# Half-height transposes and a state product on four 64x64 places of TensorE, with a new plan of PSUM banks

## The chip, the cores and the metric

One NeuronCore of a Trainium2 chip runs the whole kernel in one launch. It has five engines that run side by side and signal each other through semaphores: TensorE (matrix products, PE in the profile, its weight loads PEld), VectorE (DVE), ScalarE (ACT), GpSimd (POOL) and SyncE (SP, here for DMAs). TensorE writes only to PSUM, which has eight banks of 512 float32 values in each of 128 partitions; VectorE and ScalarE read it from there. The metric is the time of one execution on the device in microseconds; the kernel before takes 1892.21 us, median of 3 runs from 1891.94 to 1892.32.

## The reference

All data is float32. `x` has 4 sequences of 2048 tokens and 256 channels. A block with a gated linear recurrence (16 heads, state 64 x 64) is followed by a layer norm, a coupled feed-forward part with three cycles, and another layer norm:

```
xn = layernorm(x) * gamma + beta
Q, K, V = xn @ WQ.T + bQ, ...              # 16 heads of 64
gate = silu(xn @ Wg.T + bg)
h_t = alpha * h_{t-1} + k_t v_t^T ;  o_t = q_t^T h_t      # per head, over 2048 tokens
x1 = layernorm(x + x + (o * gate) @ WO.T + bO)
gf = sigmoid(mlp3(mean over tokens of x1))
out = x1
3 times: tf = sigmoid(mlp4(out)); coupling = 0.1 + range * (0.7 gf + 0.3 tf - 0.5) * 2
         out = out + coupling * twist(out)   # channel halves swapped with signs
result = layernorm(x1 + out)
```

## The kernel before

**Tiling.** Each sequence (`b`) is worked in four steps (`s`, counted through as `it`) of 512 tokens; a step is four chunks (`c`) of 128 tokens. Heads go in pairs `p` = 0 to 7; the two heads `e` of a pair lie on partitions 0 to 63 and 64 to 127. `n = it * 8 + p` counts head pairs through, 128 in all.

**A head pair** on TensorE: `project` makes keys, queries and gates of the next pair (6 matmuls of 512 columns each, float32 split into a high and a low part); `y_part` adds the output projection of the pair before; `from_state` multiplies the queries with the state at each chunk's start; `keys_transposed` turns the decayed keys `k_end` to tokens; `from_chunk` adds the masked scores times values; `updates` makes each chunk's addition to the state, of the next pair; `scores` makes the next pair's scores. Before the eight pairs, `values` projects V in eight parts. Plain float32 products run as two matmuls each, transposes as one.

**The other engines.** VectorE evacuates keys (`keys_of`, L615) and queries (`queries_of`, L624), masks the scores (`masked`, L703), runs the state from chunk to chunk (L732, L736) and multiplies the result with the gate (`gated`, L714). ScalarE makes the scaled, block-diagonal state `h_bd` (`states_of`, L454), shifted queries (L436), the gate (L428) and the copy `k_tok` of the transposed keys (L446); around the steps it scales the transposed x (L420), splits it (L423) and copies x1 (L462). GpSimd makes `k_end` (L362).

**What sets the order.** Every engine's program is written out by hand in the order in which it runs; waits are on counting semaphores, each with one meaning (`state_carried` is the last state step, `k_evacuated` the keys out of PSUM, `gate_evacuated` the gate). A bank is written again only after its reader signalled, so the plan of banks decides which waits there are. Before, keys and queries alternate between banks 0 and 1, the gate is in the keys' bank, scores are in 2 and 3, transposed keys and state updates in 4, the result of the scan in 5, the output projection in 6 and 7. x is transposed into banks 0 and 1 behind the keys of p = 6. In the feed-forward part (`order`, layers 1 to 4) L1078, L1095, L1108 and L1121 are the four layers, L934 transposes x1, and L943 turns the final sum back.

## Time and profile before

| | |
|---|---|
| median of the runs | 1892.21 us |
| profiled execution | 1892.58 us |
| its span, first to last instruction | 1890.8 us |
| mean granted TensorE clock | 0.985 of full speed |
| PE busy | 1824.6 us, 96% |
| PEld busy | 1396.9 us, 74% |
| DVE busy | 1062.4 us, 56% |
| ACT busy | 699.9 us, 37% |
| POOL busy | 312.9 us, 17% |

The busy time of an engine is the union of its instructions' times; the ends of matmuls are modelled, and they are pipelined, so that their times overlap each other. PE and PEld are the same engine, its matmuls and its weight loads. One group of the table of costliest groups is one source line with one kind of operands; it gives busy time, mean time of one instruction, and the idle time of the engine ahead of them. The chain that ended last runs 94% over PE.

### The profile page before, as it was taken

To read this page: it belongs to the slowest core of one execution; us is meant where nothing else is said; L and a number is where in the kernel's file an instruction comes from. 1 tells how busy PE (TensorE), PEld (TensorE's weight loads), DVE (VectorE), ACT (ScalarE), POOL (GpSimd) and SP (SyncE) were. 2 spreads that over 40 slices of the span, in tenths; PEclk is the share of its full clock that TensorE was granted. 3 is DMA by queue.
4 is the path that set the end of the run, shared out by engine and by line. 5 is a ranking of instruction groups with operands and counts; after the bars stand their busy time and mean duration, and the time that the engine had idled before them with its cause. 6 is when DMAs were issued, how large, how long until landed. Compare 5 with 4: busy or idle time off the path is not lost.

```text
span 1890.8 us, 43949 instructions
## 1 busy us (share of the span) xinstructions
PE 1824.6 (96%) x19120; PEld 1396.9 (74%) x19120; DVE 1062.4 (56%) x2214; ACT 699.9 (37%) x1282; POOL 312.9 (17%) x244
## 2 busy tenths in 40 slices
PE   5999999999899999999989999999989999999996
PEld 4888888863588888885368888888437888888732
DVE  7565555555745555554665645555565555555556
ACT  3323333344433333334433332323443333233344
POOL 4121211102212121110221112121022111212002
PEclk8999999999899999999989999999999999999998
DMA  4000000000100000000010000000001000000001
GB/s 161 2 13 2 13 2 12 2 1 1 56 2 13 2 12 2 12 2 1 0 57 2 13 2 13 2 13 2 1 1 57 2 13 2 13 2 2 2 0 45
DMA packets 22817, 26.11 MB, mean 14 GB/s; under 512 B 3169, under 2 KB 21473, under 8 KB 22625
## 3 DMA queue, kind: packets, MB, share of 16 engines
q1 hardware_dynamic: 20624, 19.09, 3.2%
q10 hardware_dynamic: 2000, 4.20, 0.6%
q8 instruction: 152, 2.49, 0.6%
q14 instruction: 41, 0.33, 0.1%
HBM read 14.90 MB, written 8.39 MB: 12 GB/s over the span
## 4 chain that ended last, share of the span: by engine, by line
PE 94%; DVE 3%; ACT 2%; POOL 1%; issue 0%; DMA 0%; ACTq 0%; DVEq 0%; SPq 0%
PE bank L848 39%; PE bank L923 12%; PE bank L1078 9%; PE bank L911 7%; PE bank L875 6%; PE bank L902 6%; PE bank L1095 4%; PE bank L892 3%; PE bank L884 3%; PE bank L1121 1%; PE bank L1108 1%; DVE stats L582 1%; PE bank L839 1%; DVE v_sb L816 1%; PE bank L934 1%; DVE x_nf L809 1%
## 5 line engine op out<-in xcount | busy, mean ns | idle before, releaser
L714 DVE TENSOR_TENSOR o_g<-bank,gate 128x512 f32<-128x512 f32 x128 | 88.6, 692 | 484.6 <-PE bank L911 484.6
L362 POOL TENSOR_TENSOR k_end<-k_sc,pows 128x512 f32<-128x512 f32 x128 | 134.9, 1054 | 1075.6 <-DVE k_sc L615 1075.6
L436 ACT ACTIVATE q_sb<-q_sb,pows 128x384 f32<-128x384 f32 (+2 forms) x384 | 167.3, 498 | 331.6 <-DVE q_sb L624 331.6
L454 ACT ACTIVATE h_bd<-h_seq,pows 64x256 f32<-64x256 f32 x256 | 129.9, 507 | 323.5 <-DVE h_seq L736 320.3
L923 PE MATMUL bank<-wo,o_g 128*128 128x256 f32 x1024 | 243.5, 380 | 0.8 <-DVE o_g L714 0.8
L923 PEld LDWEIGHTS bank<-wo,o_g 128*128 128x128 f32 x1024 | 192.7, 190 | 32.9 <-DVE o_g L714 1.0
L446 ACT ACTIVATE k_tok<-bank 128x512 f32<-128x512 f32 x128 | 76.5, 598 | 299.9 <-PE bank L884 299.9
L703 DVE COPY_PREDICATED att<-causal,bank 128x1024 f32<-128x1024 int32 x128 | 167.3, 1307 | 6.2 <-PE bank L875 5.4
L911 PE MATMUL bank<-att,v_sb 128*64 128x128 f32 x2048 | 140.1, 279 | 0.0
L902 PEld LDWEIGHTS bank<-q_sb,h_bd 128*128 128x128 f32 x1024 | 134.1, 191 | 7.4 <-ACT h_bd L454 0.2
L902 PE MATMUL bank<-q_sb,h_bd 128*128 128x128 f32 x1024 | 134.9, 275 | 0.0
L875 PE MATMUL bank<-q_sb,k_sc 64*32 64x128 f32 (+3 forms) x8192 | 128.1, 236 | 0.0
L911 PEld LDWEIGHTS bank<-att,v_sb 128*64 128x64 f32 x2048 | 109.2, 136 | 24.4 <-issue 24.3
L624 DVE SCALAR_TENSOR_TENSOR q_sb<-bank,col_bias,pows 128x512 f32<-128x512 f32 x128 | 96.2, 751 | 53.9 <-PE bank L848 53.4
L736 DVE SCALAR_TENSOR_TENSOR h_seq<-h_seq,pows,bank 128x64 f32<-128x64 f32 x384 | 107.9, 281 | 24.3 <-PE bank L892 1.9
L1078 PE MATMUL bank<-v_sb,f_w 128*128 128x512 f32 x256 | 121.0, 605 | 0.0
L848 PE MATMUL bank<-x_hi,wk_hi 128*128 128x512 f32 x256 | 114.6, 448 | 0.0
L875 PEld LDWEIGHTS bank<-q_sb,k_sc 64*32 64x32 f32 x8192 | 102.1, 106 | 14.3 <-issue 5.9
L696 DVE TENSOR_TENSOR v_sb<-bank,bias_v 128x512 f32<-128x512 f32 x128 | 85.1, 688 | 47.4 <-PE bank L848 46.8
L848 PE MATMUL bank<-wv_hi,x_hi 128*128 128x512 f32 x256 | 108.5, 424 | 2.4 <-POOL wv_lo L358 1.7
L848 PE MATMUL bank<-x_hi,wq_hi 128*128 128x512 f32 x256 | 102.9, 402 | 3.4 <-DVE x_lo L610 3.4
L848 PE MATMUL bank<-x_hi,wg_hi 128*128 128x512 f32 x256 | 103.6, 405 | 2.2 <-POOL wg_lo L358 2.2
(137 smaller groups left out, 3213.6 us busy)
## 6 DMA issues: line engine op xcount, KB each, us to landing
x_in<-in_x SPq DMA_DIRECT2D x16, 512.0 KB, 4.3
out_y<-q_sb SPq DMA_DIRECT2D x8, 512.0 KB, 2.8
out_y<-x_nf SPq DMA_DIRECT2D x8, 512.0 KB, 3.1
v_sb<-in_wq ACTq DMA_DIRECT2D x1, 1024.0 KB, 5.2
v_sb<-in_wk SPq DMA_DIRECT2D x1, 1024.0 KB, 9.0
x1t<-in_wg ACTq DMA_DIRECT2D x1, 1024.0 KB, 9.4
x1t<-in_wv ACTq DMA_DIRECT2D x1, 1024.0 KB, 13.5
wo<-in_wo ACTq DMA_DIRECT2D x1, 1024.0 KB, 17.4
```

Of the source, the lines that this page charges most:

```text
L362: nc.gpsimd.tensor_tensor(k_end[:].rearrange("p (a z) (b r) -> p a (z b) r", z=2, r=BL), k_sc[:].rearrange("p (a z) (b r) -> p a (z b) r", ...
L436: last = nc.scalar.activation(q_sb[:, p % 2, d].rearrange("p (a z) n -> p a (z n)", z=2)[:, :, reach], q_sb[:, p % 2, 0].rearrange("p (a z ...
L454: nc.scalar.activation(h_bd[rows, :, e * DH:(e + 1) * DH], h_seq[rows, :, :], ACT.Copy, scale=pows[rows, p, HP:HP + 1]).then_inc(s_hbd, 1)
L624: nc.vector.scalar_tensor_tensor(q_sb[:, p % 2, 0].rearrange("p c (b r) -> p (c b) r", r=BL), bank[q_bank(p)].rearrange("p (c r) -> p c r" ...
L703: nc.vector.copy_predicated(att[:].rearrange("p e (a z) n -> p (e a) (z n)", z=2), causal[:].bitcast(i32).rearrange("p z n -> p (z n)").un ...
L736: step = nc.vector.scalar_tensor_tensor(h_seq[:, c + 1, :] if c + 1 < NC else h_st[:, p, :], h_seq[:, c, :], pows[:, p, HP + 1:HP + 2], ba ...
L848: last = nc.tensor.matmul(dst, l(k), r(k), start=(m == 0), stop=(m == 5))
L875: last = nc.tensor.matmul(bank[2 + e][g * BL:(g + 1) * BL, cols:cols + count * BL], k_sc[rows, c, g * BL:(g + 1) * BL], query_blocks(rows, ...
L902: nc.tensor.matmul(bank[5][:, c * C:(c + 1) * C], h_bd[:, c, :], query_blocks(slice(0, P), p, c, first, NB), start=(c == 0), stop=False, s ...
L911: last = nc.tensor.matmul(bank[5][e * DH:(e + 1) * DH, c * C:(c + 1) * C], v_sb[:, c, h * DH:(h + 1) * DH], att[:, e, c, :], start=False, ...
L923: last = nc.tensor.matmul(dst, o_g[:, p % 2, tok], wo[:, p, :], start=(p == 0 and c % 2 == 0), stop=(p == NP - 1), skip_group_check=True)
L1078: last = nc.tensor.matmul(l1_bank(j, m)[:], f_w1[:, k, m * P:(m + 1) * P], src[:, k, tile_cols(t)], start=(k == 0), stop=(k == KT - 1))
```

## The change

- **State product.** `from_state` multiplies 64 rows with 64 columns for each head and chunk in place of a block-diagonal 128 x 128. Head `e` of an even chunk writes partitions `e * 64` up of bank 4; in odd chunks the two heads' halves are swapped and in bank 5, so the four products of two chunks lie on the four 64x64 places of the array. The state is scaled in one activation to `h_sc`, without zero blocks. `from_chunk` writes to the same places, the gate of odd chunks is written with its halves swapped, and the output projection takes `wo` with swapped halves for them (two more DMAs of half of `wo` at the start).
- **Transposes.** Every 128 x 128 transpose becomes two of 64 rows by 128 columns (`by_halves`), row half `e` into bank `first_bank + e`; the readers take their columns from two banks.
- **Banks.** Keys, gate and one half of the transposed keys use bank 0; queries, the other half and the state updates bank 1; V uses banks 2 to 5; x is transposed into banks 2 and 3, ahead of `y_part` of p = 6.

```diff
-            return n % NP % 2 if n else 5
+            return 0 if n else 5
+        def head_half(c, e):
+            first = (e + c) % 2 * DH
+            return slice(first, first + DH)
+        def halves_of(first_bank, first, count):
+            return psum[:, first_bank:first_bank + 2, first * DH:(first + count) * DH].rearrange(
+                "p r (c n) -> p c r n", n=DH)
...
-            return bank[(2, 3, 5, 1, 2, 3, 0, 5)[m]]
+            return bank[2 + m % 4]
...
-                nc.scalar.activation(gate[:, p % 2, :], bank[g_bank(n)], ACT.Silu,
-                                     bias=col_bias[:, 2, p:p + 1]).then_inc(s_gev, 1)
+                even, odd = by_places(bank[g_bank(n)])[:, 0], by_places(bank[g_bank(n)])[:, 1]
+                nc.scalar.activation(by_places(gate[:, p % 2, :])[:, 0], even, ACT.Silu, bias=col_bias[:, 2, p:p + 1])
+                for e in range(2):
+                    rows, other = slice(e * DH, (e + 1) * DH), slice((1 - e) * DH, (2 - e) * DH)
+                    last = nc.scalar.activation(by_places(gate[other, p % 2, :])[:, 1], odd[rows], ACT.Silu,
+                                                bias=col_bias[rows, 2, p:p + 1])
+                last.then_inc(s_gev, 1)
...
-                nc.scalar.activation(k_tok[:], part(bk, NC), ACT.Copy).then_inc(s_ktok, 1)
+                nc.scalar.activation(in_halves(k_tok[:].rearrange("p c m -> p (c m)")), halves_of(0, 0, NC),
+                                     ACT.Copy).then_inc(s_ktok, 1)
...
-                for e in range(2):
-                    rows = slice(e * DH, (e + 1) * DH)
-                    nc.scalar.activation(h_bd[rows, :, e * DH:(e + 1) * DH], h_seq[rows, :, :],
-                                         ACT.Copy, scale=pows[rows, p, HP:HP + 1]).then_inc(s_hbd, 1)
+                nc.scalar.activation(h_sc[:], h_seq[:], ACT.Copy, scale=pows[:, p, HP:HP + 1]).then_inc(s_hsc, 1)
...
+                act.wait_ge(s_x1t, step + 1 + C0)
                 for k in range(KT):
-                    act.wait_ge(s_x1t, step * KT + k + 1 + C0)
...
+                            if p == NP - 2 and following:
+                                x_scaled(it + 1)
+                            tokens_of(n + 1)
...
-                nc.vector.tensor_tensor(o_g[:, p % 2], bank[5], gate[:, p % 2, :], ALU.mult).then_inc(s_og, 1)
+                nc.vector.tensor_tensor(by_places(o_g[:, p % 2]), psum[:, 4:6, 0:2 * C].rearrange("p z (a n) -> p z a n", n=C),
+                                        by_places(gate[:, p % 2, :]), ALU.mult).then_inc(s_og, 1)
...
+            def by_halves(first_bank, place, src):
+                for e in range(2):
+                    rows = slice(e * DH, (e + 1) * DH)
+                    last = nc.tensor.transpose(bank[first_bank + e][:, place * DH:(place + 1) * DH],
+                                               src[rows, :], ident[rows, rows])
+                return last
...
-                    last = nc.tensor.transpose(bank[bk][:, c * C:(c + 1) * C], k_end[:, c, :], ident[:])
+                    last = by_halves(0, c, k_end[:, c, :])
...
-                    nc.tensor.matmul(bank[5][:, c * C:(c + 1) * C], h_bd[:, c, :],
-                                     query_blocks(slice(0, P), p, c, first, NB),
-                                     start=(c == 0), stop=False, skip_group_check=True)
+                    place = slice(c // 2 * C, (c // 2 + 1) * C)
+                    for e in range(2):
+                        rows = slice(e * DH, (e + 1) * DH)
+                        nc.tensor.matmul(bank[4 + c % 2][head_half(c, e), place], h_sc[rows, c, :],
+                                         query_blocks(rows, p, c, first, NB),
+                                         start=(c < 2), stop=False, skip_group_check=True)
...
-                            pe.wait_ge(s_qev, n + 1 + C0)
-                            project("k", p + 1, k_bank(p + 1)).then_inc(s_k, 1)
-                            pe.wait_ge(s_gev, n + 1)
-                            project("q", p + 1, q_bank(p + 1)).then_inc(s_q, 1)
+                            project("k", p + 1, 0).then_inc(s_k, 1)
+                            pe.wait_ge(s_hend, n + 1 + C0)
+                            project("q", p + 1, 1).then_inc(s_q, 1)
...
+                        if p == NP - 2 and following:
+                            pe.wait_ge(s_xn, it + 2)
+                            pe.wait_ge(s_att, n + 1 + C0)
+                            x_transposed()
...
                             pe.wait_ge(s_kend, n + 2 + C0)
-                            pe.wait_ge(s_hend, n + 1 + C0)
-                            keys_transposed(4).then_inc(s_kt, 1)
+                            pe.wait_ge(s_qev, n + 2 + C0)
+                            pe.wait_ge(s_gev, n + 2)
+                            keys_transposed().then_inc(s_kt, 1)
...
-                                pe.wait_ge(s_x1c, (b + 1) * NS * KT - 1 + j + C0)
+                                pe.wait_ge(s_x1c, (b + 1) * NS * KT + C0)
```

The order of the instructions shows it at three places. A row is line, operation, output and inputs, the output's shape, the count of equal ones in a row, and the semaphores waited for. First TensorE in p = 0 of the first step, before: the ends of the key and query projections (`wk`, `wq`), the starts behind them, and what follows the gate projection (`wg`).

```order
L848 MATMUL bank<-x_hi,wk_lo 128x512
L848 MATMUL bank<-x_hi,wq_hi 128x512 [waits gate_evacuated]
L848 MATMUL bank<-x_lo,wq_hi 128x512
...
L848 MATMUL bank<-x_hi,wq_lo 128x512
L848 MATMUL bank<-x_hi,wg_hi 128x512 [waits k_evacuated]
...
L848 MATMUL bank<-x_hi,wg_lo 128x512
L902 MATMUL bank<-q_sb,h_bd 128x128 [waits o_gated,state_diagonal_ready]
L902 MATMUL bank<-q_sb,h_bd 128x128 x3
L884 MATMUL bank<-ident,k_end 128x128 [waits state_carried,k_end_ready]
L884 MATMUL bank<-ident,k_end 128x128 x3
```

The same place after:

```order
L876 MATMUL bank<-x_hi,wk_lo 128x512
L876 MATMUL bank<-x_hi,wq_hi 128x512 [waits state_carried]
L876 MATMUL bank<-x_lo,wq_hi 128x512
...
L876 MATMUL bank<-x_hi,wq_lo 128x512
L876 MATMUL bank<-x_hi,wg_hi 128x512 [waits k_evacuated]
...
L876 MATMUL bank<-x_hi,wg_lo 128x512
L933 MATMUL bank<-q_sb,h_sc 64x128 [waits o_gated,state_scaled]
L933 MATMUL bank<-q_sb,h_sc 64x128 x7
L860 MATMUL bank<-ident,k_end 128x64 [waits gate_evacuated,q_evacuated,k_end_ready]
L860 MATMUL bank<-ident,k_end 128x64 x7
```

The wait of the query projection went from the gate to the state, the key transposes wait for gate and queries instead of the state, and the state product is twice as many of half the rows. TensorE in p = 6, before, from the output projection (`wo`) to the state updates (L892):

```order
L923 MATMUL bank<-wo,o_g 128x256 [waits o_gated]
L923 MATMUL bank<-wo,o_g 128x256 x3
L902 MATMUL bank<-q_sb,h_bd 128x128 [waits o_gated,state_diagonal_ready]
L902 MATMUL bank<-q_sb,h_bd 128x128 x3
L884 MATMUL bank<-ident,k_end 128x128 [waits state_carried,k_end_ready]
L884 MATMUL bank<-ident,k_end 128x128 x3
L839 MATMUL bank<-ident,x_nf 128x128 [waits gate_evacuated,q_evacuated,x_n_ready]
L839 MATMUL bank<-ident,x_nf 128x128 x7
L911 MATMUL bank<-att,v_sb 64x128 [waits scores_masked]
L911 MATMUL bank<-att,v_sb 64x128 x7
```

After:

```order
L860 MATMUL bank<-ident,x_nf 128x64 [waits scores_masked,x_n_ready]
L860 MATMUL bank<-ident,x_nf 128x64 x15
L955 MATMUL bank<-wo,o_g 128x256 [waits o_gated]
L955 MATMUL bank<-wo,o_g 128x256 x3
L933 MATMUL bank<-q_sb,h_sc 64x128 [waits o_gated,state_scaled]
L933 MATMUL bank<-q_sb,h_sc 64x128 x7
L860 MATMUL bank<-ident,k_end 128x64 [waits gate_evacuated,q_evacuated,k_end_ready]
L860 MATMUL bank<-ident,k_end 128x64 x7
L943 MATMUL bank<-att,v_sb 64x128 [waits scores_masked]
L943 MATMUL bank<-att,v_sb 64x128 x7
```

The x transposes stand ahead of the output projection and wait for the masked scores. ScalarE in p = 0, from the state (`h_bd`, `h_sc`) to `k_tok`, before:

```order
L454 ACTIVATE h_bd<-h_seq,pows 64x4x64 [waits o_ready,state_step]
L454 ACTIVATE h_bd<-h_seq,pows 64x4x64
L436 ACTIVATE q_sb<-q_sb,pows 128x2x192 [waits q_evacuated]
L436 ACTIVATE q_sb<-q_sb,pows 128x2x128
L436 ACTIVATE q_sb<-q_sb,pows 128x2x64
L428 ACTIVATE gate<-bank,col_bias 128x512 [waits gate_projected,o_gated]
L446 ACTIVATE k_tok<-bank 128x512 [waits state_update_ready,k_end_transposed]
```

After:

```order
L471 ACTIVATE h_sc<-h_seq,pows 128x256 [waits o_ready,state_step]
L454 ACTIVATE q_sb<-q_sb,pows 128x2x192 [waits q_evacuated]
L454 ACTIVATE q_sb<-q_sb,pows 128x2x128
L454 ACTIVATE q_sb<-q_sb,pows 128x2x64
L442 ACTIVATE gate<-bank,col_bias 128x2x128 [waits gate_projected,o_gated]
L445 ACTIVATE gate<-bank,col_bias 64x2x128 x2
L464 ACTIVATE k_tok<-bank 128x512 [waits state_update_ready,k_end_transposed]
```

One activation makes the state where two did, and three the gate where one did.

## Rows read from the trace of the kernel before

**Rows 1.** Page, part 1: engine, busy us (share), instructions.
```profile
PE 1824.6 (96%) x19120; PEld 1396.9 (74%) x19120; DVE 1062.4 (56%) x2214; ACT 699.9 (37%) x1282; POOL 312.9 (17%) x244
```

**Rows 2.** Waits table: engine, line, awaited; us in total, times, longest.
```profile
PEld bank L848 <- DVE k_sc L615: 8.4, 23, 0.4
```

**Rows 3.** Timeline, head pair p = 5: start us, us, engine, line, shapes, count.
```profile
190.20 1.89 PE L923 MATMUL bank<-wo,o_g 128*128 128x256 f32 x8
191.00 0.67 ACT L428 ACTIVATE gate<-bank,col_bias 128x512 f32<-128x512 f32 x1
...
191.92 1.05 PE L902 MATMUL bank<-q_sb,h_bd 128*128 128x128 f32 x8
...
192.81 0.60 PE L884 MATMUL bank<-ident,k_end 128*128 128x128 f32 x4
...
193.34 1.09 PE L911 MATMUL bank<-att,v_sb 128*64 128x128 f32 x16
193.45 0.60 ACT L446 ACTIVATE k_tok<-bank 128x512 f32<-128x512 f32 x1 [1.78 <-PE bank L884]
194.16 0.60 PEld L892 LDWEIGHTS bank<-v_sb,k_tok 128*64 128x64 f32 x16
194.27 0.63 PE L892 MATMUL bank<-v_sb,k_tok 128*64 128x64 f32 x16
```

**Rows 4.** Groups by shape: busy us, mean ns of one, idle before.
```profile
L703 DVE COPY_PREDICATED att<-causal,bank 128x1024 f32<-128x1024 int32 x128 | 167.3, 1307 | 6.2 <-PE bank L875 5.4 <-issue 0.2
...
L902 PE MATMUL bank<-q_sb,h_bd 128*128 128x128 f32 x1024 | 134.9, 275 | 0.0
...
L892 PE MATMUL bank<-v_sb,k_tok 128*64 128x64 f32 x2048 | 82.1, 222 | 2.3 <-ACT k_tok L446 2.3
...
L884 PE MATMUL bank<-ident,k_end 128*128 128x128 f32 x512 | 76.8, 273 | 0.0
...
L436 ACT ACTIVATE q_sb<-q_sb,pows 128x256 f32<-128x256 f32 x128 | 63.0, 492 | 0.0
L884 PEld LDWEIGHTS bank<-ident,k_end 128*128 128x128 f32 x512 | 60.7, 141 | 2.2
...
L436 ACT ACTIVATE q_sb<-q_sb,pows 128x128 f32<-128x128 f32 x128 | 49.4, 386 | 0.0
...
L1121 PEld LDWEIGHTS bank<-x_2b,f_w 64*128 64x128 f32 x96 | 7.2, 184 | 21.9 <-issue 15.2 <-ACT x_2b L541 6.7
```

**Rows 5.** Timeline: the scores, eight places of 64x32.
```profile
205.55 1.00 PE L875 MATMUL bank<-q_sb,k_sc 64*32 64x128 f32 x64
```

**Rows 6.** Timeline: row halves side by side, then transposes without and with a change.
```profile
203.09 1.04 PE L839 MATMUL bank<-ident,x_nf 128*128 128x128 f32 x8
...
419.26 0.30 PEld L1121 LDWEIGHTS bank<-x_2b,f_w 64*128 64x128 f32 x4 [0.76 <-issue]
419.26 1.13 PE L1121 MATMUL bank<-x_2b,f_w 64*128 64x512 f32 x4
...
482.24 1.09 PE L943 MATMUL bank<-ident,v_sb 128*128 128x128 f32 x8
```

**Rows 7.** Timeline, head pair p = 0.
```profile
231.09 0.40 PE L848 MATMUL bank<-x_hi,wq_hi 128*128 128x512 f32 x1
...
231.61 1.04 ACT L454 ACTIVATE h_bd<-h_seq,pows 64x256 f32<-64x256 f32 x2 [5.67 <-DVE h_seq L736]
231.61 0.28 DVE L736 SCALAR_TENSOR_TENSOR h_st<-h_seq,pows,bank 128x64 f32<-128x64 f32 x1
...
233.54 1.31 ACT L436 ACTIVATE q_sb<-q_sb,pows 128x384 f32<-128x384 f32 x3 [0.89 <-DVE q_sb L624]
...
233.87 0.39 PE L848 MATMUL bank<-x_hi,wg_lo 128*128 128x512 f32 x1
...
234.76 0.67 ACT L428 ACTIVATE gate<-bank,col_bias 128x512 f32<-128x512 f32 x1
...
234.99 0.60 PE L884 MATMUL bank<-ident,k_end 128*128 128x128 f32 x4
```

More of the change, by code:

```diff
@@ L98, in build @@
         h_seq = sb("h_seq", [P, NC, DH])
-        h_bd = sb("h_bd", [P, NC, P])
+        h_sc = sb("h_sc", [P, NC, DH])
         o_g = sb("o_g", [P, 2, ST])
@@ L838, in x_transposed @@
                     for c in range(NC):
[L839 to L841 removed]
+                        last = by_halves(2, k * NC + c, x_n[:, c, k * P:(k + 1) * P])
+                last.then_inc(s_xt, 1)
             def products(dst, first, end, l_hi, l_lo, r_hi, r_lo):
@@ L922, in y_part @@
                     dst = bank[6 + c // 2][:, (c % 2) * D:(c % 2 + 1) * D]
-                    last = nc.tensor.matmul(dst, o_g[:, p % 2, tok], wo[:, p, :], start=(p == 0 and c % 2 == 0),
+                    last = nc.tensor.matmul(dst, o_g[:, p % 2, tok], wo[:, c % 2, p, :], start=(p == 0 and c % 2 == 0),
                                             stop=(p == NP - 1), skip_group_check=True)
@@ L933, in x1_transposed @@
                     for c in range(NC):
-                        last = nc.tensor.transpose(bank[first_bank + k][:, c * C:(c + 1) * C],
-                                                   x_n[:, c, k * P:(k + 1) * P], ident[:])
-                    last.then_inc(s_x1t, 1)
+                        last = by_halves(first_bank, k * NC + c, x_n[:, c, k * P:(k + 1) * P])
+                last.then_inc(s_x1t, 1)
             def final_transposed(b, t):
```

123 lines of the change are left out of this document (57 added, 66 removed).

## The prediction

> **What bounds the kernel now.** I read the page's first lines, then the waits, then the order of time inside one head pair, then the groups by shape. TensorE's matmuls are busy 1824.6 of 1890.8 us [rows 1]. That alone proves little, since the ends of pipelined matmuls are modelled, so the waits come next: the largest wait of TensorE on another engine inside the scan is its weight load waiting for the evacuated keys, 8.4 us in 23 places [rows 2]. So in the eight head pairs of each 512-token step TensorE works without a gap, and a microsecond taken from it is won unless another engine's result then comes late. The timeline shows the stretch that changes, in the usual head pair (p = 1 to 5) [rows 3]: `y_part` (L923), product with the state (L902), transposed keys (L884), product with the masked scores (L911), state update (L892). Each starts before the modelled end of the one ahead. ScalarE's gate (ends 191.67) has more than a microsecond before the transposes; its `k_tok` (ends 194.05) has only 0.1 us before L892's weights load (194.16).
>
> **Step times.** From the timeline and the means by shape [rows 3, 4]: L902 is 8 matmuls in 1.05 us, so (1.05 - 0.275) / 7 = 0.111 us from start to start; L884 (0.60 - 0.273) / 3 = 0.109 us for 128 columns; L892, two column places side by side, (0.63 - 0.22) / 7 = 0.058 us per pair of 64 columns; L911, also two places, 0.109 us per pair of 128 columns. Time thus goes with the columns streamed, and places run side by side: with eight places 64 matmuls take 1.00 us [rows 5], 16 ns apart on average. A change of tile shape costs: within one shape the next group starts 0.16 us before the modelled end of the last (L902 ends 192.97, L884 starts 192.81), across shapes only 0.07 us before (L884 ends 193.41, L911 starts 193.34), and its first weight load is uncovered. An uncovered load of a plain 128-column operand is 0.11 us (the second pair of L1121's loads starts 0.30 - 0.184 = 0.11 us after the first [rows 4, 6]). A transpose's load is shorter, 141 ns against the 184 of L1121's 128 columns [rows 4], and uncovered it costs 0.05 us (L943 behind a change of shape 1.09 us, L839 without one 1.04, both 8 transposes [rows 6]); a 64-column load is the same 0.05.
>
> **The state product, 128 times.** Before, 4 block-diagonal products are 8 matmuls, 8 x 0.111 = 0.89 us. Now 8 products of 64x64 are 16 matmuls on four places: four rounds of 0.109 us = 0.44. Against that stands a change of shape ahead of it. On the clock of the timeline [rows 3]: `y_part` ends 192.09, weights load 192.02, streaming from 192.07, last round starts 192.40; before, the last started 192.70 (192.97 less 0.27). That is 0.29 us. No row has four such places with two of different row halves in one bank; the bounds are 0.29 gained and, if they run two at a time (0.87 us), 0.15 lost. I take the gain, by the eight places [rows 5].
>
> **The halved transposes.** The keys are 8 half transposes in pairs on the two row halves, writing two banks. L1121 is the nearest row: its two row halves run side by side, 4 matmuls of 512 columns in 1.13 us. Each half streams 64 columns, and a transpose's load is about 0.05, so a pair costs 0.058 us by L892. There is a second change of shape: load 192.62, streaming 192.67, last pair starts 192.85 and ends 193.07, L911 streams from 193.05. Before it streamed from 193.39. So the usual head pair gains 0.34 us, 0.29 of it from the product and 0.05 from the transposes. The other end of the unknown is a pair at 0.11, the pace of L1121's 128-column loads (4 in 0.30 us at 184 ns each): then the usual pair gains only 0.09. The Trainium skill, "TensorE: Matmul & The Clock Gate", section on LDWEIGHTS, says that a load takes its columns / 1.2, the same for a transpose. By that rule it would be the 0.11. The 0.05 us of L943 speaks against it [rows 6].
>
> **The waits that move.** In the order of the instructions the key transposes now wait for the evacuated gate, since both use bank 0, and the query projection waits for `state_carried`, since bank 1 also holds the update. In p = 1 to 6 the query projection starts after the last state step, at no cost. The gate is now three activations on 256 columns. One is 0.67 us less 256 columns at 0.83 ns, 0.455 us (the slope from 386 and 492 ns of L436 at 128 and 256 columns [rows 4]). The two `h_bd` halves of 507 ns need 1.04 us [rows 7], so activations that change their partitions do not overlap; 3 x 0.455 + 0.06 = 1.42 us. Gate from 191.00 ends 192.42, the transposes' weights are wanted at 192.62: hidden with 0.15 us left. `h_sc` is one activation in place of two: ScalarE is relieved by 0.5 us there, off the path. `k_tok`'s chain keeps its 0.1 us.
>
> At p = 0 neither wait is hidden. VectorE masks first there and runs the state steps second, so the last one ends 231.89 [rows 7], while the query projection started at 231.09; with 0.04 us for the signal (L884 ends 193.41, L446 starts 193.45 [rows 3]) and the uncovered load it streams from 232.05, 0.96 us later. The gate projection then no longer waits for the keys (at most 0.4 us of idle loads [rows 2], 0.23 of it felt by the matmuls), so its last matmul starts 0.73 later, 234.60 instead of 233.87. The shifts sit idle until VectorE has evacuated the queries [rows 7], and that follows the projection; both come 0.89 later (0.96, less 0.07 by which VectorE's own keys held up the queries before), so the gate starts at 235.65 instead of 234.76 and ends 237.07. And p = 0 has no `y_part` between gate projection and transposes: TensorE is ready for them at 235.53 and waits until 237.12, 1.6 us. Their last pair then starts 237.36 where the last key transpose started 235.31, 2.04 us late. In 12 steps 8 transposes of `x1` follow (0.46 us instead of 0.87): 1.58 lost each; in the 4 steps without them 1.99. Sum 12 x 1.58 + 4 x 1.99 = 27.0 us.
>
> **The rest.** p = 7 (16 times) has no key transposes, a plain projection follows with its uncovered load: gain 0.09 x 15 + 0.29 = 1.6. The x transposes (15 times) move from behind the keys to between gate projection and `y_part`: two changes of shape and 8 pairs are 0.82 us where 0.87 were, gain 0.06 x 15 = 0.9. They also wait for the mask, done 2 us before, and ScalarE's two copies come before `k_tok`, ending just as the keys are transposed. The first keys of a step, between value projections (16 times): two changes added, 0.82 - 0.68 = 0.14 x 16 = 2.3 lost. In the feed-forward part layer 2 waits for both `x1t` copies, 0.5 x 4 = 2.1 lost, and the first final transposes give 0.25 x 4 = 1.0. The batch's start waits for VectorE's final statistics either way: nothing. Two more loads of `wo` at the start are needed only at p = 1: nothing.
>
> **Sum.** 96 pairs x 0.34 = 32.7 + 1.6 + 0.9 + 1.0 = 36.2 gained; 27.0 + 2.3 + 2.1 = 31.4 lost; net -4.8 us. The profiled execution took 1892.58 us (span 1890.8), the median is 1892.21, so 1887.8 against the first and 1887.4 against the second. By its own unknowns (0.1 us in each p = 0 chain is 1.6 us, 0.05 us in each pair 5) this is 1879 to 1896. About 0.2%, 3.8 us, is what a measurement tells from no change, so the sum lies just beyond it.
>
> **The rivals.** (a) Late readers: VectorE's chain from the gated output through state steps and mask to the keys has no room (it already stops the weight load in 23 places [rows 2]), and `k_tok` has 0.1 us. Both now read two banks in short runs. For: no slack. Against: the mask reads two banks already, 1307 ns for 1024 columns [rows 4], and shows no penalty for it that stands out. It decides from 0.03 us on; 0.15 us per read costs (0.15 - 0.03) x 112 = 13 us: 1901, slower. (b) Half transposes at 0.11 a pair: 96 x 0.25 + 16 x 0.25 x 2 + 31 x 0.43 = 24 + 8 + 13 = 45 lost: 1932. (c) The four places don't overlap in full: 112 x 0.44 = 49 lost: 1936. The Trainium skill, "TensorEngine Tiling (Array Packing)", section on PSUM pressure, says that different row tiles cannot use one PSUM bank at a time, and here two on the diagonal do. By that rule this rival holds. The row halves of L875 and L1121 always write different banks [rows 5, 6], so no row here shows it either way. (d) The p = 0 waits don't bind: without the 27.0 and with 16 x 0.34 + 12 x 0.41 = 10 more, 1850.
>
> **Chances.** Sum 0.66; (a) 0.14; (b) 0.07; (c) 0.06; (d) 0.07. Within the sum 60% lie below 1888.4, 30% within 0.2%, 10% above. Faster 0.66 x 0.6 + 0.07 = 0.47; same 0.66 x 0.3 + 0.14 x 0.3 = 0.24; slower the rest, 0.29. The range takes in the sum's own and (a), with five microseconds more at each end for the terms that lie behind them, and leaves out (b), (c) and (d): 1874 to 1906.
>
> **What would show it.** Right: 16 matmuls of the state product in about 0.7 us; 8 half transposes of keys in about 0.45; the product with the scores 0.34 us earlier behind `y_part`; at p = 0 about 1 us of waiting ahead of the query projection for VectorE and 1.6 ahead of the key transposes for ScalarE's gate, together some 40 us of waits in the table that had 8. Wrong: a state product over 1 us (c), transposes over 0.6 (b), waits for keys or `k_tok` in all head pairs (a), no waits at p = 0 (d).

## The result: slower by half a per cent

The changed kernel takes 1900.38 us (median of 8 runs, 1898.23 to 1905.40), the kernel before 1892.09 (8 runs, 1891.88 to 1892.32). The ratio is 1.0048, 95% interval 1.0037 to 1.0060. The forecast was 1887.4; the time lies inside the range but on the other side of no change. The profiled execution of the changed kernel took 1899.36 us, 6.8 more than the one of before; the account below is of these two executions, and the medians lie 8.3 us apart. The runs of the changed kernel also lie seven microseconds apart where before they lay within half a microsecond.

Of the page of the changed kernel, its first lines:

```profile
span 1897.6 us, 47887 instructions
PE 1774.2 (93%) x21040; PEld 1290.3 (68%) x21040; DVE 1060.0 (56%) x2211; ACT 728.1 (38%) x1410; POOL 312.8 (16%) x244
```

TensorE is busy 50 us less than in [rows 1], and the span is 7 us longer: the work became shorter, and by the modelled ends 57 us more of standing still came in. The table of TensorE's waits, against [rows 2], says where:

```profile
PE bank L860 <- ACT gate L445: 31.0, 16, 3.1
...
PE bank L876 <- DVE h_st L757: 11.2, 16, 0.7
PE bank L876 <- DVE x_lo L630: 8.3, 1, 8.3
...
PEld bank L876 <- DVE h_st L757: 18.2, 16, 1.2
...
PEld bank L876 <- DVE k_sc L635: 3.1, 20, 0.2
```

Each line gives the wait's total, how often it came and the longest, in us. L860 is now every transpose, L876 every projection. The lines for the gate (31.0 us) and the state `h_st` (11.2 us) are the two waits of p = 0, once in each of the 16 steps; the one for `x_lo` comes once, at the start. The wait for the evacuated keys, 8.4 us in [rows 2], is down to 3.1, and no line of the table waits for `k_tok`.

**The usual head pair.** The timeline of p = 5 in the second step, the place of [rows 3] (start, duration, engine):

```profile
186.07 0.43 PEld L933 LDWEIGHTS bank<-q_sb,h_sc 64*64 64x64 f32 x16 [0.33 <-issue]
186.07 0.67 PE L933 MATMUL bank<-q_sb,h_sc 64*64 64x128 f32 x16
186.67 0.33 PEld L860 LDWEIGHTS bank<-ident,k_end 64*128 64x128 f32 x8 [0.17 <-issue]
186.67 0.47 PE L860 MATMUL bank<-ident,k_end 64*128 64x64 f32 x8
187.07 1.09 PE L943 MATMUL bank<-att,v_sb 128*64 128x128 f32 x16
187.17 0.60 ACT L464 ACTIVATE k_tok<-bank 128x512 f32<-128x512 f32 x1 [0.69 <-PE bank L860]
187.99 0.64 PE L920 MATMUL bank<-v_sb,k_tok 128*64 128x64 f32 x16
188.56 1.00 PE L903 MATMUL bank<-q_sb,k_sc 64*32 64x128 f32 x64
```

Sixteen matmuls of the state product take 0.67 us where eight took 1.05, and eight half transposes 0.47 us where four whole ones took 0.60. The product with the scores starts 1.00 us behind the start of the state product; in [rows 3] it was 1.42 us. `k_tok` ends 0.1 us ahead of the update's weights, as before.

**p = 0.** The same view of the first head pair of the third step, lines between left out:

```profile
232.12 1.31 DVE L723 COPY_PREDICATED att<-causal,bank 128x1024 f32<-128x1024 int32 x1 [0.34 <-PE bank L903]
...
234.55 0.28 DVE L757 SCALAR_TENSOR_TENSOR h_st<-h_seq,pows,bank 128x64 f32<-128x64 f32 x1
...
234.89 0.51 PE L876 MATMUL bank<-x_hi,wq_hi 128*128 128x512 f32 x1 [0.70 <-DVE h_st L757]
...
236.66 0.75 DVE L644 SCALAR_TENSOR_TENSOR q_sb<-bank,col_bias,pows 128x512 f32<-128x512 f32 x1 [1.17 <-PE bank L876]
...
237.45 1.31 ACT L454 ACTIVATE q_sb<-q_sb,pows 128x384 f32<-128x384 f32 x3 [2.39 <-DVE q_sb L644]
237.55 0.39 PE L876 MATMUL bank<-x_hi,wg_lo 128*128 128x512 f32 x1
...
237.87 0.67 PE L933 MATMUL bank<-q_sb,h_sc 64*64 64x128 f32 x16
238.66 0.45 ACT L442 ACTIVATE gate<-bank,col_bias 128x256 f32<-128x256 f32 x1
239.13 0.95 ACT L445 ACTIVATE gate<-bank,col_bias 64x256 f32<-64x256 f32 x2
...
240.22 0.46 PE L860 MATMUL bank<-ident,k_end 64*128 64x64 f32 x8 [1.69 <-ACT gate L445]
```

In order of time the path runs: mask, state steps, query projection, evacuated queries, shifts, gate, transposes. From the gate projection's last matmul (237.55) on, the path runs over ScalarE alone; TensorE does the state product and then stands for 1.69 us.

**Sums by head pair.** From the starts of the state updates in both timelines, the change of each interval from one update to the next (us, summed over the 16 steps; the column "7 and phase" also holds the projection of V for the next step and, three times, the feed-forward part):

| to first update | p=0 | 1 | 2 | 3 | 4 | 5 | 6 | 7 and phase | after the last update |
|---|---|---|---|---|---|---|---|---|---|
| +3.0 | +32.6 | -2.8 | -5.4 | -5.7 | -5.6 | -5.7 | -5.9 | +2.2 | 0.0 |

One ordinary interval is 0.33 us shorter; p = 0 is 1.74 to 1.79 longer in the twelve steps that are not a batch's first, and 2.14, 3.71, 2.66 and 2.85 longer in the four that are. The sum is +6.7 us. That is the whole account of the two profiled executions (6.8 us), and its large entries, the first two columns, were then tested by themselves.

### The profile page after: what moved, and what is told of

Read it like the earlier page. It is cut to its first block, busy times and chain, and to the rows that moved or that the text cites. A ratio compares the mean times of both kernels' runs of the same rounds, so it can differ in the third digit from the quotient of the medians.

```text
span 1897.6 us, 47887 instructions
## 1 busy us (share of the span) xinstructions
PE 1774.2 (93%) x21040; PEld 1290.3 (68%) x21040; DVE 1060.0 (56%) x2211; ACT 728.1 (38%) x1410; POOL 312.8 (16%) x244
## 4 chain that ended last, share of the span: by engine, by line
PE 88%; DVE 6%; ACT 4%; issue 1%; ACTq 1%; DMA 0%; DVEq 0%
PE bank L876 36%; PE bank L955 12%; PE bank L1104 9%; PE bank L943 7%; PE bank L903 6%; PE bank L1121 4%; PE bank L860 4%; PE bank L933 4%; PE bank L920 3%; PE bank L1147 1%; PE bank L1134 1%; DVE att L723 1%; DVE stats L602 1%; ACT q_sb L454 1%; ACT gate L445 1%
## 5 line engine op out<-in xcount | busy, mean ns | idle before, releaser
L471 ACT ACTIVATE h_sc<-h_seq,pows 128x256 f32<-128x256 f32 x128 | 65.3, 510 | 331.0 <-DVE h_seq L757 331.0
L723 DVE COPY_PREDICATED att<-causal,bank 128x1024 f32<-128x1024 int32 x128 | 167.5, 1309 | 5.9 <-PE bank L903 5.9
L876 PE MATMUL bank<-x_hi,wq_hi 128*128 128x512 f32 x256 | 104.7, 409 | 19.4 <-DVE h_st L757 11.2
L445 ACT ACTIVATE gate<-bank,col_bias 64x256 f32<-64x256 f32 x256 | 120.0, 469 | 3.2
L876 PE MATMUL bank<-x_hi,wk_hi 128*128 128x512 f32 x256 | 114.9, 449 | 0.0
L876 PE MATMUL bank<-wv_hi,x_hi 128*128 128x512 f32 x256 | 108.0, 422 | 5.0 <-ACT x_nf L576 1.9
L876 PE MATMUL bank<-x_hi,wg_hi 128*128 128x512 f32 x256 | 101.6, 397 | 2.4 <-POOL wg_lo L369 2.4
L635 DVE SCALAR_TENSOR_TENSOR k_sc<-bank,col_bias,pows 128x512 f32<-128x512 f32 x128 | 94.8, 740 | 15.8 <-PE bank L876 15.8
```

Source lines behind the costliest of these rows:

```text
L445: last = nc.scalar.activation(by_places(gate[other, p % 2, :])[:, 1], odd[rows], ACT.Silu, bias=col_bias[rows, 2, p:p + 1])
L635: nc.vector.scalar_tensor_tensor(k_sc[:].rearrange("p c (b r) -> p (c b) r", r=BL), bank[0].rearrange("p (c r) -> p c r", r=BL), col_bias[ ...
L723: nc.vector.copy_predicated(att[:].rearrange("p e (a z) n -> p (e a) (z n)", z=2), causal[:].bitcast(i32).rearrange("p z n -> p (z n)").un ...
L876: last = nc.tensor.matmul(dst, l(k), r(k), start=(m == 0), stop=(m == 5))
```

## The experiments

Each ran in several rounds beside the kernel before, whose medians were 1891.78 to 1891.88. W is the theory that the loss sits in the start and in p = 0; the other letters are explained where they stand.

**1. The extra loads of `wo`.** In the changed kernel:

```diff
-            for e in range(2):
-                act.dma_start(wo[(1 - e) * DH:(2 - e) * DH, 1], ...).then_inc(s_wo, 16)
...
             for dst, src in consts:
                 sp.dma_start(dst, src).then_inc(s_const, 16)
+            for e in range(2):
+                sp.dma_start(wo[(1 - e) * DH:(2 - e) * DH, 1], ...).then_inc(s_wo, 16)
```

> The changed kernel, with its two extra half loads of `wo` issued by SyncE behind all its other loads instead of by ScalarE. Theory Q (the start's 3.0 us are ScalarE's queue, which stands at the two issues until 17.9 us, while the first x transposes are ready at about 14): the scaled x starts at about 14.0 us instead of 18.0, the first state update 3.0 us earlier, the whole 3.0 us less than the changed kernel, about 1897.4. Rival B (the start is late since 1 MB more is in flight on the DMA engines and everything lands later): nothing comes back, 1900.4.

Measured 1895.01 us (1891.64 to 1900.64). In the changed kernel ScalarE's start reads:

```profile
7.18 0.49 ACTq L497 DMA_DIRECT2D wo<-in_wo  x1
7.70 10.19 ACTq L499 DMA_DIRECT2D wo<-in_wo  x2
18.02 1.45 ACT L430 ACTIVATE x_nf<-bank,beta,gamma 128x512 f32<-128x512 f32 x2 [9.91 <-issue]
```

and with the loads on SyncE:

```profile
13.83 1.45 ACT L433 ACTIVATE x_nf<-bank,beta,gamma 128x512 f32<-128x512 f32 x2 [5.84 <-PE bank L860]
```

The activation is the same; what ended the idle time ahead of it is its own queue in one case and TensorE's transposes in the other. Theory Q holds: 4.2 us at the start of this profile (first update at 44.0 us instead of 48.2). The median fell by 5.4 us and not by 3.0; the time to the first update and the clock's falls (below) both vary from run to run, and how much of the rest is due to which is not shown.

**2. The same loads in the kernel before**, and nothing else:

```diff
+            for e in range(2):
+                act.dma_start(wo[(1 - e) * DH:(2 - e) * DH, 1], ...).then_inc(s_wo, 16)
```

> The kernel before, with nothing but the changed kernel's two extra half loads of `wo` on ScalarE (into a second half of the tile that is not read). Theory Q: ScalarE's queue stands at them for some 10 us, the scaled x starts at 18 us instead of 14, the first state update 2.5 to 3.5 us later: 1895.0. Rival: the first x transposes were late in the changed kernel for another reason (their new form, or one copy per two banks), and the loads alone cost nothing: 1892.

Measured 1895.14 us, ratio 1.0018 (1.0009 to 1.0026). ScalarE's scaled x starts at 17.17 us instead of 14.04, the two loads hold its queue for 8.96 us, and no interval between updates differs by more than 0.01 us on average. So the loads alone cost 3.3 us of the median (1.9 at the first update of this profile). With run 1 it shows that where they are issued decides, not the new form of the x transposes.

**3. State steps ahead of the mask at p = 0.**

```diff
-                        if p == 0:
-                            masked(n)
-
                         dve.wait_ge(s_hsc, n + C0)
...
                         if p + 1 < NP:
-                            if p:
-                                masked(n)
+                            masked(n)
                             keys_of(p + 1, n + 1)
```

> The changed kernel, with VectorE's state steps ahead of its mask at p = 0, as they already are in the other head pairs. Theory W (the loss sits in the two waits of p = 0; the first is the query projection's wait for `state_carried`, which comes 1.3 us of mask too late): the wait of the projections for L757 (11.2 us on the matmuls) falls to almost nothing, all that follows at p = 0, the gate too, comes 1.0 us earlier, 16 x 1.0 = 16 us less: 1884.5. Rival R (VectorE is as late one step on: the mask now delays the evacuated keys, and the gate projection or the gate waits for that): half or less comes back, 1892 to 1900.

Measured 1885.03 us. `state_carried` no longer shows among TensorE's matmul waits, and p = 0 is 0.82 us longer than before instead of 1.77: 0.96 us less in an ordinary step, and 0.93 to 0.98 less in a batch's first. Theory W holds, and rival R is out.

**4. The gate of p = 0 through bank 2.**

```diff
-            return 0 if n else 5
+            return 5 if n == 0 else 2 if n % NP == 1 else 0
...
+                            if p == 0:
+                                pe.wait_ge(s_att, n + 1 + C0)
                             project("g", p + 1, g_bank(n + 1)).then_inc(s_g, 1)
...
-                            pe.wait_ge(s_gev, n + 2)
+                            if p:
+                                pe.wait_ge(s_gev, n + 2)
                             keys_transposed().then_inc(s_kt, 1)
...
+                            if p == 0:
+                                pe.wait_ge(s_gev, n + 2)
                             scores(p + 1).then_inc(s_score, 1)
```

ScalarE makes `k_tok` ahead of this gate.

> The changed kernel, with the gate projection made at p = 0 put into bank 2 (free between two masks) instead of bank 0, and ScalarE's `k_tok` ahead of that gate, so that the key transposes of p = 0 wait for nobody's gate; the next scores wait for it instead. Theory W: ScalarE's 31 us of waits ahead of the transposes go, 1.6 us in 12 steps less 0.35 that the scores then wait for the gate, and 2.0 to 3.3 in 4 less 0.8 to 2.1: 12 x 1.25 + 4 x 1.2 = 20 us less, 1880.5. The half clock behind the waits at 520 and 1452 us should go too. Rival R (the wait only moves to the scores and to `k_tok`): 10 us or less comes back, 1890 or more.

Measured 1875.20 us. In a step that is not a batch's first:

```profile
145.01 0.46 PE L863 MATMUL bank<-ident,k_end 64*128 64x64 f32 x8
...
146.05 0.47 ACT L442 ACTIVATE gate<-bank,col_bias 128x256 f32<-128x256 f32 x1
146.53 0.95 ACT L445 ACTIVATE gate<-bank,col_bias 64x256 f32<-64x256 f32 x2
...
147.63 0.99 PE L906 MATMUL bank<-q_sb,k_sc 64*32 64x128 f32 x64 [0.18 <-ACT gate L445]
```

The transposes wait for nothing, and the gate is late for the scores by 0.18 us, not the 0.35 I had worked out. p = 0 becomes 1.75 us shorter and p = 1 takes 0.23 back: 1.52 us a step instead of the 1.25 expected. In the 12 ordinary steps that is 3 of the 5 us by which the 25 us exceed the 20; for the rest, the clock fell once in this profile and not twice (below).

**5. The three together.**

> The three edits together: extra `wo` loads on SyncE, state steps ahead of the mask at p = 0, gate of p = 0 in bank 2. Theory W: the three are independent, 3 + 16 + 20 = 39 us less than the changed kernel, about 1861, and so some 31 us (1.6%) under the kernel before, close to the 36 us that the 128 head pairs gain less the small losses. Rival R: the waits stand in for one another, 1875 to 1885.

Measured 1864.59 us, 36 less than the changed kernel, where 39 were expected. The edits almost add up. At the first step of batches 2 to 4 a loss stayed, and the next run takes 1.4 us from each of them.

**6. Silu's table early**, on top of the three, at the end of a batch:

```diff
+                if b + 1 < B:
+                    nc.scalar.activation(warm[:], logit[:, 0:1], ACT.Silu)
```

> The three edits of before, and one more: at the end of each batch but the last ScalarE applies Silu to one column that nobody reads, so that the 1.28 us load of its function table (in the trace ahead of the first gate of batches 2 to 4) comes there and not between the shifts and the gate. Theory W: the p = 0 and p = 1 intervals of these three batch starts (1.33, 1.30 and 1.33 us over an ordinary step's, after taking 1.4 off where the clock fell) lose 1.3 us each, and no clock drop follows at 968 us: 3.9 to 5.3 us less than with the three edits, about 1860. Rival T (the table load is hidden anyway, or only moves to a place that waits as well): 1864.

Measured 1857.48 us, 7.1 less than with the three edits, where 3.9 to 5.3 were expected. In the changed kernel the fifth step, a batch's first, reads:

```profile
517.66 1.28 ACT L442 ACT_TABLE_LOAD   x1
518.95 0.47 ACT L442 ACTIVATE gate<-bank,col_bias 128x256 f32<-128x256 f32 x1
519.44 0.95 ACT L445 ACTIVATE gate<-bank,col_bias 64x256 f32<-64x256 f32 x2
...
520.53 0.69 PE L860 MATMUL bank<-ident,k_end 64*128 64x64 f32 x8 [3.10 <-ACT gate L445]
```

The feed-forward part ends with other functions, so the first Silu of a batch loads its table, on the path. With the load moved, p = 0 and p = 1 together take 1.4 us less at each of the three starts: with the three edits they were 0.81 us over the kernel before where the clock stayed whole, and now they are 0.59 under it. The fall of the clock in the profile with the three edits (1.4 us) is gone too, which makes 5.6 us. The first update came 1.2 us earlier in this profile, which is no more than it varies without cause (last section).

**7. The same in the kernel before.**

> The kernel before, with nothing but the early load of Silu's table at the end of the first three batches. Theory W: the first p = 0 interval of the program, whose table came long before, is not on record as shorter, but in the changed kernel with three edits the three later batch starts gave back 1.4 us each, of which only 0.5 to 0.65 were new against the kernel before; so its own table load costs the kernel before about 0.8 us a batch start: 2.4 us less, 1889.5. Rival: in the kernel before the table load lies beside TensorE's work in full, 1891.9.

Measured 1889.38 us, ratio 0.9988 (0.9980 to 0.9997). Each of the three p = 0 intervals is 0.92 us shorter, all others unchanged. So the load was never hidden in full; before, 0.9 of its 1.28 us were on the path already. The sign of it stood in [rows 4], in the 2.3 us that L892 waited for `k_tok`; the table of waits of the kernel before says how often:

```profile
PE bank L892 <- ACT k_tok L446: 2.3, 3, 0.8
```

The three waits stand at 516.6, 980.8 and 1444.4 us, each in a batch's first step.

**8. Early table alone in the changed kernel.**

> The changed kernel with nothing but the early load of Silu's table. Theory W: at the three batch starts the gate's way lies open there, so the whole 1.28 us of the load goes, 3.8 us in a run in which the clock falls as before: 1896.5. Theory K (clock): the 3.4 us falls of the granted clock come only behind the longest p = 0 waits (3.1 us at the batch starts, 1.9 in the other steps) and cost 1.3 us each; with the longest wait down to 1.9 there is at most one of them and the runs lie closer together: 1894.5, spread under 3 us. If the falls come with waits of 1.9 us as well, the spread stays at 7 us.

Measured 1893.42 us (1890.53 to 1897.76). The waits for the gate fell from 31.0 to 26.7 us and the longest from 3.1 to 1.7, as W says. Theory K fails in its condition: the spread stayed at seven microseconds, and the profile shows four falls of the clock, one at each batch's start, behind waits of 1.7 us. The median is 7.0 us under the changed kernel's, though, and W alone allows 3.8. The profiled execution is the slowest of the eleven (1897.76), and the median of the granted clocks is 0.986 against 0.984 in the changed kernel, so the falls seem to have become rarer without going away.

**9. Keys in full height.** In the changed kernel:

```diff
                 for c in range(NC):
-                    last = by_halves(0, c, k_end[:, c, :])
+                    last = nc.tensor.transpose(bank[0][:, c * C:(c + 1) * C], k_end[:, c, :], ident[:])
```

> The changed kernel with the keys alone transposed in full height again (4 transposes into bank 0, k_tok read from that bank). Theory S (time goes with streamed columns, a pair of halves takes 0.058 us, a change of tile shape comes either way): 4 x 0.109 in place of 4 x 0.058 us, +0.21 us in 112 head pairs and in 16 first keys: +27 us, 1927. So the halves pay for the shape change that the four places bring, rather than being a second cost. Rival L (a pair of halves is bound by its weights' loads and costs what one full transpose costs, the changed kernel gaining by the state product alone): no difference, 1900.

Measured 1927.49 us, ratio 1.0189 (1.0175 to 1.0203).

```profile
187.51 0.67 PE L932 MATMUL bank<-q_sb,h_sc 64*64 64x128 f32 x16
188.11 0.66 PE L911 MATMUL bank<-ident,k_end 128*128 128x128 f32 x4
188.70 1.09 PE L942 MATMUL bank<-att,v_sb 128*64 128x128 f32 x16
```

From the transposes' start to the next product it is 0.59 us instead of 0.40, and an ordinary interval is 0.14 us shorter than before instead of 0.33. So theory S holds for the head pairs, and rival L is out. The first keys of a step, between two value projections, went the other way: with full height their interval is 0.14 us shorter, as the prediction had it, where this expectation had added 0.21. That the time still comes out at 1927 is luck: the intervals with the clock whole give some 21 us, and the rest goes with the clock, which fell eight times in this profile and twice in the changed kernel's.

**10. Two places.** In the changed kernel, without the exchange of halves (with one gate activation as in the next run, and `wo[:, 0]` alone read):

```diff
-            first = (e + c) % 2 * DH
+            first = e * DH
```

> The changed kernel without the exchange: the halves of each state product and of each product with the scores stay on their own rows, so only two of the four 64x64 places (those on the diagonal) are used, two at a time in one bank; the gate is then one activation and only one arrangement of `wo` is read (the extra loads are still made). Theory F (four places run at once, 4 rounds of 0.109 us against 8 on two): the state product takes about 1.1 us from first to last end instead of 0.67, +0.44 x 128 = 56 us, less 11.7 for the single gate at p = 0: 1944. Rival P (a 64-row product is cheap by its shape, not by its place): 1888.5.

Measured 1935.46 us, ratio 1.0230 (1.0216 to 1.0244).

```profile
188.33 1.09 PE L928 MATMUL bank<-q_sb,h_sc 64*64 64x128 f32 x16
189.35 0.46 PE L855 MATMUL bank<-ident,k_end 64*128 64x64 f32 x8
```

The same sixteen matmuls take 1.09 us from the diagonal alone and 0.67 on all four places; every pair but p = 0 is 0.43 us longer than in the changed kernel. Theory F. The expectation was 8 us too high, mostly since it charged the 0.44 at p = 0 too, where the state product lies ahead of the wait for the gate and costs nothing (p = 0 is as long here as in run 11): 112 x 0.43 - 16 x 0.75 = +36 us, 1936.

**11. One gate activation.** Left out is the exchange of the gate's halves:

```diff
-                nc.scalar.activation(by_places(gate[:, p % 2, :])[:, 0], even, ACT.Silu, ...)
-                for e in range(2):
-                    ...
-                    last = nc.scalar.activation(by_places(gate[other, p % 2, :])[:, 1], odd[rows], ACT.Silu, ...)
-                last.then_inc(s_gev, 1)
+                nc.scalar.activation(gate[:, p % 2, :], bank[g_bank(n)], ACT.Silu,
+                                     bias=col_bias[:, 2, p:p + 1]).then_inc(s_gev, 1)
```

> The changed kernel with the gate as one activation of 512 columns; left out is the exchange of its halves in odd chunks, so the gate meets the wrong head there. Theory W: at p = 0 the gate stands on the path and becomes 0.69 us instead of 0.47 + 0.48 + 0.47 = 1.42, so 0.73 x 16 = 11.7 us less, 1888.5; in the other head pairs nothing. Rival G (the gate's three parts also hold up k_tok or the state's scaling in every head pair): 0.1 us or more from each of 96 pairs on top, under 1879.

Measured 1885.85 us. p = 0 is 0.75 us shorter in every step (12.0 us), the other intervals the same. Theory W holds; G is out. The profiled executions lie 13.0 us apart, and what they have beyond the 12.0 is one fall of the clock less, with the start 0.5 us later; that the 14.5 us between the medians hold the same is likely, not shown.

**12. The best version.** The four edits, with full height for the first keys of a step and, at a batch's end, for x1:

```diff
+                    if whole:
+                        last = nc.tensor.transpose(bank[0][:, c * C:(c + 1) * C], k_end[:, c, :], ident[:])
...
+                if first_bank == 4:
+                    for k in range(KT):
+                        for c in range(NC):
+                            last = nc.tensor.transpose(bank[4 + k][:, c * C:(c + 1) * C],
+                                                       x_n[:, c, k * P:(k + 1) * P], ident[:])
+                        last.then_inc(s_x1k, 1)
...
-                                pe.wait_ge(s_x1c, (b + 1) * NS * KT + C0)
+                                pe.wait_ge(s_x1c, (b + 1) * NS * KT - 1 + j + C0)
```

> The four edits (wo on SyncE, state steps first, gate of p = 0 in bank 2, table early), and besides the two places where the halves were forecast to cost: the first keys of a step transposed in full height (between two value projections, 0.14 us x 16 = 2.2 us by the forecast and by the run with all keys in full height), and in the last step of a batch x1 in full height too, one plane per bank, so that each of layer 2's products waits for one copy only (0.5 us x 4 by the forecast). Theory: 2.2 + 2.0 = 4.2 us less than with four edits, 1853.3. Rival: the batch end is bound by ScalarE or VectorE whichever way x1 comes, 1855.3.

Measured 1852.59 us (1852.49 to 1852.75), ratio 0.9793 (0.9779 to 0.9806): 39.2 us (2.1%) under the kernel before and 47.8 under the changed one. The expectation was 4.2 us under run 6, and it is 4.9: 0.16 us at each of the first keys, and some 0.5 us at each batch's end. What is left of its waits at p = 0:

```profile
PE bank L917 <- ACT gate L450: 4.7, 16, 0.7
PE bank L890 <- DVE k_sc L653: 3.1, 16, 0.2
```

## Why the prediction was wrong

**What was right.** The head pair: 0.34 us forecast, 0.33 measured, with the state product at 0.67 us (forecast 0.7) and the transposes at 0.47 (0.45). A pair of half transposes starts 0.061 us behind the one ahead of it, close to the 0.058 taken and far from 0.11: rival (b) is out. Rival (c) is out too: a round of four products of L933 starts every 0.109 us. The Trainium skill, "TensorEngine Tiling (Array Packing)", section on PSUM pressure, says that different row tiles cannot use one bank at the same time. Here the diagonal pairs of L933 do write one bank each; if one of a pair had waited for the other, only two products could have run at a time, one in each bank, and the four places would not have beaten the 1.09 us of run 10. The 0.67 us disagrees with that rule. Rival (a) is out: the gated output stays at 692 ns, `k_tok` at 598, the mask at 1309, and no head pair but p = 0 is late. Rival (d) is out, since both waits of p = 0 bind; run 3 took 0.96 us from each step, the very value forecast for the first.

**How the 0.34 splits** was stated as 0.29 for the product and 0.05 for the transposes. As steps on TensorE's timeline that is so: from the end of the output projection the last round of the product starts 0.29 us earlier than before, and the product with the scores 0.33. As edits it is not: run 9 shows that four places with full-height keys win 0.14, and the halved keys 0.19 more. With full-height keys behind the four places the transposes pay for the change of tile shape, 0.59 us to the next product against 0.53 before; with halved keys that cost comes as well, but it is there already.

**What failed.** The change does bring its gain in the usual head pair and lose in p = 0, but the forecast's -4.8 us was the small difference of 36.2 gained and 31.4 lost, and the loss was put too low in these terms. Against -4.8 the profiled execution shows +6.8, a miss of 11.6 us:

| term | forecast | measured | miss |
|---|---|---|---|
| two more loads of `wo` at the start | 0 | +3.0 | 3.0 |
| p = 0, 12 ordinary steps | 1.58 each | 1.77 each | 2.3 |
| p = 0, 4 first steps of a batch, clock whole (the 2.63 is run 1's) | 1.99 each | 2.14, and 3 x 2.63 | 2.1 |
| falls of the clock at two batch starts | none | +1.5, +1.4 | 2.9 |
| p = 1 in two steps | none | +0.85, +0.25, not explained | 1.1 |
| all other terms together | | | 0.2 |

*"Two more loads of `wo` at the start are needed only at p = 1: nothing."* Had this cost and the clock's falls not come, the time would have been 0.9 us over the kernel before, which is no change and still no gain. The step asked when the data are needed and not what queues behind the instructions that fetch them. They stand in ScalarE's queue, which held there for 10.19 us, and the scaled x waited behind them. Run 1 takes the loads away from that queue and run 2 puts them alone into the kernel before, and they show it from both sides.

*"1.58 lost each."* It is 1.77. The mechanism is the one forecast, and its first half is exact. Against the chain of [rows 7], moved to the same state steps, the gate projection ends where forecast (within 0.01 us), the evacuated queries and with them shifts and gate come 0.07 later, and from the gate's end to the first transpose it is 0.14 us where I had taken 0.05 for signal and load. Together that is 0.16 of the 0.19 us missed in a step. The estimate took each signal at its shortest; why the handovers take longer here is not shown.

*"In the 4 steps without them 1.99."* The gate's arrival was read from a step in the middle of a batch [rows 7] and used for its first step as well, where a 1.28 us table load lies between shifts and gate in batches 2 to 4, and they lost 2.63 us with the clock whole. The kernel before pays 0.92 us for the load (run 7), which the difference does not show; the change exposes the rest of it, and run 6 gets it back.

**The clock.** A fall of TensorE's clock was in no term. This is the fifth step's p = 0 in the changed kernel. A row is a stretch, its length, the busy times of PE, PEld, DVE, ACT and POOL with their instructions, then the granted clock (1.00 is 2.4 GHz, 0.50 is 1.2), and last the share and rate of the DMAs:

```profile
516.90:520.40 3.50, 0.53 (x16) 0.29 (x14) 0.00 (x0) 3.43 (x7) 0.00 (x0) 1.00 0.00 0
520.50:523.80 3.30, 3.27 (x40) 3.17 (x40) 0.62 (x2) 0.60 (x1) 0.00 (x0) 0.50 0.02 5
523.90:527.30 3.40, 3.40 (x77) 2.82 (x76) 3.17 (x7) 0.51 (x1) 0.00 (x0) 1.00 0.00 0
```

TensorE works 0.53 us of 3.5, ScalarE throughout; then the clock is 0.50 for 3.4 us, and the intervals of p = 0 and p = 1 together take 1.4 to 1.5 us longer. The kernel before has no such stretch at a batch's start. The same place of run 8:

```profile
518.20:521.60 3.40, 1.74 (x35) 1.33 (x36) 0.00 (x0) 2.73 (x7) 0.00 (x0) 1.00 0.00 0
521.70:525.10 3.40, 3.40 (x90) 3.12 (x86) 2.14 (x7) 0.56 (x2) 0.00 (x0) 0.50 0.02 5
```

and of run 6, where the wait ahead of the transposes is gone:

```profile
505.50:508.90 3.40, 2.73 (x104) 2.45 (x103) 1.58 (x5) 1.90 (x4) 0.00 (x0) 1.00 0.00 0
509.00:512.40 3.40, 3.40 (x34) 2.68 (x17) 2.49 (x4) 0.50 (x1) 0.72 (x1) 1.00 0.02 5
```

The runs of one kernel differ by how often it happens: run 1's eight go from 1891.64 us at a mean granted clock of 0.987 over 1895.26 at 0.984 and 1897.66 at 0.982 to 1900.64 at 0.979. The profiled execution of the changed kernel shows two such falls, those of runs 1 and 10 two each, of run 8 four, of run 9 eight, of runs 3, 4, 5 and 11 one each, of runs 6 and 12 none, as in the kernel before and in runs 2 and 7. Of the versions of the changed kernel, runs 6 and 12 are also those that repeat within half a microsecond. So a wait in the midst of full work of TensorE can cost more than its length, and it makes a kernel noisy. The length of the wait alone does not decide: in the changed kernel a wait of 3.12 us at 986 us was followed by no fall, in run 8 each of the four waits of 1.7 us in a batch's first step was and none of the twelve equal ones in the other steps, and in run 9 six of those were. What decides stays open.

## What to carry to other kernels

A wait that the change adds is not judged in the steady state alone: walk through the first and last pass of every loop (here p = 0 and a batch's first step) with the order that the other engines have there, and look for what happens only then, a function table above all. A DMA costs the engine that issues it, at the place where it is issued, whenever its data are needed: here the same two loads held ScalarE's queue for 9 to 10 us ahead of the scaled x, and behind SyncE's other loads they cost nothing that shows. When a change wins on the bounding engine and the total does not move, the win is mostly there still: sums by pass of the loop show in which pass it is given back, and here three small edits in that pass and one at the start brought 43 us over the changed kernel.

## What the runs showed of the hardware

- Four 64x64 places of TensorE work at once, two of them into one bank: 16 matmuls of 128 columns take 0.67 us, against 1.09 us with two places (run 10).
- A half transpose (64 rows in, 64 columns out) on each row half takes about 0.06 us for the pair, the pace of L892's pairs of 64 columns, though its weights are 128 columns wide; ahead of the second pair behind a change of tile shape it is 0.11.
- Two loads of 512 KB, with 64 partitions and rows of 1 KB each, hold ScalarE's queue for 8.96 us (run 2) and 10.19 us (changed kernel) at the start, while other loads are in flight; one of 1 MB ahead of them holds it 0.49 us. On SyncE, from 21.09 us on, the same two hold their queue for 3.28 us (run 1). Why they hold it is not tested.
- The load of Silu's table takes 1.28 us and starts only behind the last activation ahead of it (517.66 us, behind the shifts' end), though ScalarE had stood idle for 2.39 us before the shifts.
- The time to the first state update varies by 1 us and more between profiles (47.2 to 48.7 us in the kernels with the loads on ScalarE, 44.0 to 45.5 in the others), which is why one profile's start is worth 3.0 here and 4.2 there.
